# Moving one small TensorE transpose and its vector copy ahead of the projections, and writing the vector engine's two halves of a layernorm as one loop

## The reference

```python
xn = _layernorm(x, axis=-1)
x = x + _L0_attn_ref(xn, ...) + _L0_ffn_ref(xn, ...)
xn = _layernorm(x, axis=-1)
x = x + _L1_attn_ref(xn, ...) + _L1_ffn_ref(xn, ...)
# layers 2 and 3 likewise

# _L1_attn_ref, what the stage around the change prepares:
q = x @ Wq + bq
k = x @ Wk + bk
v = x @ Wv + bv
alpha = jax.nn.sigmoid(x @ Wa + ba)
beta = jax.nn.sigmoid(x @ Wb + bb)
gate = jax.nn.sigmoid(x @ Wg + bg)
# then a gated delta rule, step by step over 256 positions, and y = o @ Wo + bo

# _L1_ffn_ref: top-1 routing to 8 experts with a capacity; dropped tokens go to expert 0
final_e = _route(tokens, router_w)
for e in range(E):
    h = jax.nn.relu(tokens @ W1[e] + b1[e])
    y = h @ W2[e] + b2[e]
    out = out + jnp.where((final_e == e)[:, None], y, 0.0)
```

## Time and profile before

| what | value |
|---|---|
| median of the runs | 704.36 us |
| the three runs | 696.79, 704.61, 704.36 us |
| the profiled execution's own time | 696.79 us |
| its span, first to last instruction | 695.1 us |
| what lies around the span | 1.7 us |
| mean granted TensorE clock | 0.961 of full speed |
| instructions | 9324 |

### The profile page before, as it was taken

The page is one execution under the profiler, slowest core; times in us unless marked ns, Lnnn a source line. Parts: engine busy times, 40 slices in busy tenths (PEclk is TensorE's granted clock), DMA queues, the critical chain, the costliest instruction groups (busy, mean ns, idle before and its releaser), DMA issues. The chain is left out here.

```text
span 695.1 us, 9324 instructions
## 1 busy us (share of the span) xinstructions
PE 593.8 (85%) x3108; PEld 395.0 (57%) x3108; DVE 464.7 (67%) x816; ACT 385.2 (55%) x798; POOL 372.0 (54%) x290
## 2 busy tenths in 40 slices
PE   5999888799898996776697759896999989898887
PEld 2433444355464553555456637896889867555546
DVE  6798699899899986974455497642335655355633
ACT  3689799779898853242579834322212346323350
POOL 0678598989999872875510172957305710112220
PEclk9999799999999999999799998999999999999999
DMA  4043154346577402000240011416013100000002
GB/s 119 4 117 61 30 122 79 113 117 129 119 121 136 121 8 69 0 0 1 81 127 1 1 25 23 137 46 172 21 39 71 32 1 1 0 1 0 1 0 62
DMA packets 45673, 40.14 MB, mean 58 GB/s; under 512 B 12167, under 2 KB 32569, under 8 KB 45626
## 3 DMA queue, kind: packets, MB, share of 16 engines
q1 hardware_dynamic: 44602, 37.45, 23.4%
q0 software_dynamic: 1024, 2.10, 1.0%
HBM read 33.44 MB, written 6.09 MB: 57 GB/s over the span
## 5 line engine op out<-in xcount | busy, mean ns | idle before, releaser
L407 PE MATMUL bank<-l0s_ring,all_ident 128*128 128x512 f32 x256 | 121.0, 606 | 2.6 <-POOL l0s_ring L661 2.6
L792 DVE TENSOR_TENSOR_SCAN l0s_ring<-l_XM,l0s_carry,bank 128x512 f32<-128x512 f32 x62 | 74.6, 1258 | 8.1 <-PE bank L390 7.3
L661 POOL TENSOR_TENSOR l0s_ring<-l0s_ring,l0s_c_rest 128x1024 f32<-128x1024 f32 x32 | 67.9, 2137 | 14.0 <-DVE l0s_ring L792 9.6
L407 PEld LDWEIGHTS bank<-l0s_ring,all_ident 128*128 128x128 f32 x256 | 46.4, 195 | 48.7 <-issue 41.0
L548 ACT ACTIVATE all_XNT<-l_wraw,l_wins 128x256 f32<-128x256 f32 x160 | 67.8, 495 | 9.6 <-PE bank L390 9.5
L661 POOL TENSOR_TENSOR l0s_ring<-l0s_ring,all_XF 128x1024 f32<-128x1024 f32 x31 | 64.2, 2082 | 8.0 <-DVE l0s_ring L792 7.3
L390 PEld LDWEIGHTS bank<-all_ident,all_XNT 128*128 128x128 f32 x320 | 37.7, 143 | 31.9 <-issue 17.6
L527 ACT ACTIVATE l_XM<-l_DT,l_negA 128x512 f32<-128x512 f32 x80 | 52.7, 709 | 0.0
L390 PE MATMUL bank<-all_ident,all_XNT 128*128 128x128 f32 x320 | 43.6, 278 | 7.9 <-ACT all_XNT L548 4.7
L792 DVE TENSOR_TENSOR_SCAN l0s_ring<-bank,l0s_carry,l0s_ring 128x512 f32<-128x512 f32 x34 | 41.8, 1263 | 1.8 <-POOL l0s_ring L651 1.8
L651 POOL TENSOR_TENSOR l0s_ring<-l_DTU,l0s_b_all 128x1024 f32<-128x1024 f32 x19 | 38.0, 1999 | 0.0
(11 more groups left out here) (421 smaller groups left out, 1498.6 us busy)
## 6 DMA issues: line engine op xcount, KB each, us to landing
l0s_c_rest<-bc_rows SPq DMA_DIRECT2D x16, 512.0 KB, 5.6
all_XF<-bc_rows SPq DMA_DIRECT2D x16, 512.0 KB, 5.5
l0s_b_all<-bc_rows SPq DMA_DIRECT2D x19, 256.0 KB, 6.6
l_wall<-in_L_ffn_W SPq DMA_DIRECT2D x14, 256.0 KB, 4.6
all_X<-in_L_attn_x SPq DMA_DIRECT2D x4, 256.0 KB, 3.7
gx<-l1m_TD SPq DMA_DIRECT2D x1, 1024.0 KB, 5.6
gy<-l1m_TD SPq DMA_DIRECT2D x1, 1024.0 KB, 8.5
out<-all_X SPq DMA_DIRECT2D x4, 256.0 KB, 2.3
```

The source lines that it names most:

```text
L407: last = nc.tensor.matmul(bank_y[j][:, :], S.ident[:, :], hc[n % CRING][:, j, :], start=False, stop=(n % DS == DS - 1))
L661: nc.gpsimd.tensor_tensor(hc[n % CRING][:, :, :], h[n % RING][:, :, :], wide(c_wide[p % HRING][:, n % 2, :]), ALU.mult).then_inc(hc_ready, 1)
L792: nc.vector.tensor_tensor_scan(h[n % RING][:, j, :], factor, added, before, ALU.mult, ALU.add).then_inc(h_ready, 1)
```

## The change

On TensorE the transpose of the expert bias rows moves, with its two waits, ahead of `turn(0)`. On VectorE the helper functions go; the two halves are one loop, in which each half does its additions, its moments and its scale and shift before the next half begins. The copies of the router weights and of the wide bias now stand inside half 0, between its moments and its shift. The copy of the expert bias leaves the loop of 16 additions and stands ahead of it.

```diff
@@ block.tensor
                         nc.tensor.matmul(S.bank[6][:, 0:KVC], S.ones[0:1, :], brow[0:1, :], start=True, stop=True).then_inc(wide, 1)
+                        pe.wait_ge(E.zero_loaded, 80)
+                        pe.wait_ge(bwide_ready, 1)
+                        nc.tensor.transpose(bank_b[:, 0:NE * FE], brows, S.ident[0:NE * FE, 0:NE * FE]).then_inc(b_turned, 1)
                         turn(0)
                         turn(1)
                         pe.wait_ge(x_ready, NBLK)
...
                         keys(1)
-                        pe.wait_ge(E.zero_loaded, 80)
-                        pe.wait_ge(bwide_ready, 1)
-                        nc.tensor.transpose(bank_b[:, 0:NE * FE], brows, S.ident[0:NE * FE, 0:NE * FE]).then_inc(b_turned, 1)
                         turn(3)
@@ block.vector
-                        add_rows(0)
-                        add_rows(1)
-                        moments(0)
-                        add_rows(2)
-                        shifts(0)
-                        add_rows(3)
-                        moments(1)
-                        dve.wait_ge(rw_turned, 1)
-                        nc.vector.tensor_copy(wt[:, KVC - NE:KVC], S.bank[7][:, 0:NE]).then_inc(wt_ready, 1)
-                        dve.wait_ge(wide, 1)
-                        nc.vector.tensor_copy(bwide, S.bank[6][:, 0:KVC]).then_inc(bwide_ready, 1)
-                        shifts(1)
+                        for h in range(2):
+                            for b in (2 * h, 2 * h + 1):
+                                dve.wait_ge(add_turned, b + 1)
+                                nc.vector.tensor_tensor(S.X[:, quads(b), :], S.X[:, quads(b), :], S.bank[b][:, :].rearrange("p (k d) -> p k d", k=TPB),
+                                                        ALU.add).then_inc(x_ready, 1)
+                            for b in (2 * h, 2 * h + 1):
+                                dve.wait_ge(x_ready, b + 1)
+                                for t in range(b * TPB, (b + 1) * TPB):
+                                    last = nc.vector.bn_stats(stats[:, t, :], S.X[:, t, :])
                             last.then_inc(stats_ready, 1)
                             dve.wait_ge(stats_ready, h + 1)
...
                             last.then_inc(moments_ready, 1)
+                            if h == 0:
+                                dve.wait_ge(rw_turned, 1)
+                                nc.vector.tensor_copy(wt[:, KVC - NE:KVC], S.bank[7][:, 0:NE]).then_inc(wt_ready, 1)
+                                dve.wait_ge(wide, 1)
+                                nc.vector.tensor_copy(bwide, S.bank[6][:, 0:KVC]).then_inc(bwide_ready, 1)
                             dve.wait_ge(root_ready, h + 1)
...
+                        dve.wait_ge(b_turned, 1)
+                        nc.vector.tensor_copy(E.b1[:, :], bank_b[:, 0:NE * FE]).then_inc(b_ready, 1)
                         dve.wait_ge(bwide_ready, 1)
                         for t in range(CH):
-                            if t == 2 * TPB:
-                                dve.wait_ge(b_turned, 1)
-                                nc.vector.tensor_copy(E.b1[:, :], bank_b[:, 0:NE * FE]).then_inc(b_ready, 1)
                             dve.wait_ge(kv_done, t + 1)
```

More of the change, by code:

```diff
@@ L1605, in moments @@
                             last.then_inc(moments_ready, 1)
-                        def shifts(h):
+                            if h == 0:
[3 more added lines that the diff above has]
+                                nc.vector.tensor_copy(bwide, S.bank[6][:, 0:KVC]).then_inc(bwide_ready, 1)
                             dve.wait_ge(root_ready, h + 1)
```

## The result

| | before | after |
|---|---|---|
| median over 22 runs each | 699.20 us | 703.53 us |
| lowest and highest | 694.47 and 708.26 | 699.43 and 707.31 |
| the profiled execution | 696.79 (span 695.1) | 705.77 (span 704.0) |
| mean granted TensorE clock there | 0.961 | 0.944 |

The ratio is 1.0065, with a 95% interval from 1.0044 to 1.0087. That is +4.5 us on 699.2 (between 3.1 and 6.1): slower, and within the 2% that I called no change. The forecast was +4.7 us on 704.36, a ratio of 1.0067.

A forecast was written before the change was run, and what follows sets the result against it. The stage was taken as bound first by loads and layernorm, then by TensorE's projections. copy_x(0) later +4.30, transpose gone -0.24, clock +0.6 gave +4.7 us on 704.36: 709.0 us, range 701 to 714.

The forecast's parts named there:

- VectorE's hold: VectorE's shift of half 0, behind two copies' waits: ScalarE starts normalising 3.58 us later; alone it makes copy_x(0) 2.98 later.
- TensorE's wait: Bias transpose ahead of turn(0) waits for all five expert loads until 348.07; copy_x(0) 4.30 us later, overlapping VectorE's delay.
- the rival of an early release: Five expert loads land before TensorE's tiles are ready at 346.61; VectorE's hold decides, +3.3 us, median 707.7; chance 0.10.
- The transpose taken out of the stream: Between keys(1) and turn(3) TensorE loses the 0.24 us transpose, in a stretch without a gap: -0.24 us.
- The clock: TensorE's clock steps to full 4.7 us after it resumes, at 352.8; 1.1 us more at half speed, about +0.6 us.
- The case of a clock low on into the router's part: Clock stays low into the router's part, 10 of 125 us after 357: over 2% slower (14.1 us); chance 0.04.
- Passing on: Behind the stage no wait absorbs the delay; +4.7 us passes on whole, the profiled execution going from 696.79 to 701.5.
- The case of time given back by the clock: Later clock falls at L1283 and L2613 miss TensorE's work, giving back 3.6 us: +0.5 us, median 704.9; chance 0.12.
- The absolute time: Whole kernel: median of the runs shown 704.36 + 4.7 = 709.1, predicted as 709.0 us; the forecast's chance 0.68.
- The low end of my range: Whole kernel: 701 us, if the runs after lie at the level of the profiled execution with +4.7.

The follow-up runs named there:

- e2: Changed kernel with TensorE's order put back, leaving VectorE's part alone; ratio to before 1.0038 (1.0006 to 1.0071).
- e3: Changed kernel with the bias rows' load on its own semaphore, TensorE's transpose waiting for that load and bwide_ready; ratio to before 1.0041 (1.0005 to 1.0077).
- e1: Kernel before with TensorE's part alone: bias transpose and its two waits ahead of turn(0); ratio to before 1.0058 (1.0024 to 1.0091).
- e6: Changed kernel with TensorE also waiting for 16 very small later loads ahead of the bias transpose; ratio to before 1.0063 (1.0039 to 1.0086).
- a1_null_after: Changed kernel run again with no edit; ratio to before 1.0096 (1.0073 to 1.0119).
- n1_null: Kernel before run again with no edit; ratio to before 0.999 (0.995 to 1.003).
- e4: Kernel of e1 with the bias rows' load on its own semaphore, VectorE's order of before; ratio to before 1.000 (0.997 to 1.003).
- e10: Kernel of e3 with GpSimd's addition at L1238 waiting for half 1's shift; ratio to before 1.0048 (1.0020 to 1.0076).
- e9: Kernel before with q and g loads and the bias rows' load on own semaphores, first matmuls waiting for nine loads; ratio to before 0.999 (0.996 to 1.002).
- e7: Kernel of e3 with the two copies moved behind half 0's shift; ratio to before 1.0070 (1.0033 to 1.0107).

## Why the prediction was right in the change and wrong in the time

**VectorE's hold (forecast: ScalarE starts 3.58 later; 2.98 alone).** Shown. ScalarE's start is +8.72 in the changed kernel, 3.49 later than the 5.23 of before. Alone it moves `copy_x(0)` by 2.8 (e2, e3).

**TensorE's wait (forecast: release at 348.07, `copy_x(0)` 4.30 later, hiding VectorE's hold).** Shown. The release is at +12.09 against the +11.92 forecast, and `copy_x(0)` is 4.46 later against 4.30. e1 gives the same without VectorE's part, e3 takes it away with the loads, e6 makes it longer with a later load. The load into `KD` took 5.2 us from issue to landing in the changed kernel. The prediction's estimate of 2.2 us from the Trainium skill (DMA: Bandwidth & Descriptors, section "Anatomy of one DMA — SWDGE (gpsimd) path") does not hold for this load, which SyncE issues at the end of a series, and the rival of an early release falls with it. (Counted from the start of each issue, as the rows are, the estimate for all loads would have been 345.7 and not 346.2; that changes nothing.) The row of the DMA issues of the changed kernel (KB, us from issue to landing), for the earlier trace rows:

```profile
l1at_KD<-in_L_attn_bo SPq DMA_DIRECT2D x1, 64.0 KB, 5.2
```

**The transpose taken out of the stream (forecast: -0.24).** From `copy_x(0)` to the stage's end it is 11.07 after and 11.43 before: -0.36, which is 0.12 more than forecast. In the second pair of profiles (a1_null_after, n1_null) it is 12.37 and 12.60: -0.23.

**The clock (forecast: +0.6).** This term was mis-sized: in the pair of profiles it is 0. I had counted the step from TensorE's release (4.7 us before, so 4.7 after); in the changed kernel it came 3.56 after the release, as early behind `copy_x(0)` as before. In the other profiles of the same two kernels it came 2.4 us later (n1_null, 4.6 behind `copy_x(0)`) and 2.6 us later (a1_null_after, 4.8). From `copy_x(0)` to the end the four profiles take 11.43 and 12.60 (before), 11.07 and 12.37 (after). So it moves from run to run by more than the term, and neither pair shows it moving with the change. The case of a clock low on into the router's part did not occur.

**Passing on (forecast: whole).** The measured +4.5 us (3.1 to 6.1) against +4.10 in the stage agrees. So do most of the other kernels: the stage is longer than n1_null's by 4.38 (e1), 2.86 (e2), 2.47 (e3), 0.78 (e4), 2.26 (e10) and -0.90 (e9), and the ratios on 723 us give 4.2, 2.7, 3.0, 0.1, 3.5 and -0.9. For e7 it is 2.65 against 5.1 (2.4 to 7.7), and e6 goes the other way against a1_null_after, as said there. It is not shown by single profiles, since the rest varied between 337.5 and 343.9 on one kind of chip and between 359.5 and 365.3 on the other, without any order in the edits. The case of time given back by the clock cannot be told from that either: it would be an average over runs, and that average gave nothing back.

**The absolute time (forecast 709.0, measured 703.53).** The sum was +4.7 and the measurement +4.5. That they are 0.2 apart is partly luck: the stage has +4.10, and the interval is 3 us wide. The step that failed is the base: "I add the same to the median". I took the 7.57 us between the profiled execution and the median of the three runs shown as a property of the kernel. Over 22 runs the median of before is 699.20, 2.4 above the profiled execution, and two of the three runs happened to lie in the upper part of a spread of 694 to 708. Read against 699.20, my 709.0 is 1.4% slower, twice what was measured. 699.20 + 4.7 = 703.9 would have been the forecast. The low end of my range, 701, stood for runs at the level of the profiled execution; the measured ones lie between that and my base. With three runs of 696.8, 704.6 and 704.4 the right thing was to say that the base is uncertain by some 8 us and to carry the change as a difference.

## What to carry to other kernels

A wait on a shared count waits for everything in it. Before an instruction is moved up in an in-order list, ask which loads its semaphore counts beyond the one that it reads, and look for another engine that waits on the same count: its release time is the time of the new wait. Two holds that meet at one instruction don't add, but each stays when the other is repaired (VectorE's hold in e3, where TensorE's wait is repaired; TensorE's wait in e1, where VectorE's hold is; in e7 the shift inside GpSimd's addition takes the hold's place), so one repair alone may give nothing. And forecast a difference, over a base from as many runs as there are: the spread of a single kernel was three times this effect.

## What the runs showed of the hardware that I had not expected

**An addition on GpSimd holds up small VectorE instructions.** A SCALAR_TENSOR_TENSOR of 128x8 numbers in SBUF takes 0.17 us, but 1.60, 1.53 and 2.18 us where it fell into GpSimd's addition of 2.35 us (e2, e3, e7), and each time it ended within 0.02 us of it. The addition lost nothing by it. Moving the addition away gave 0.17 back (e10). A RECIPROCAL inside the same addition (352.52 in e2) kept its 0.20. The Trainium skill (SBUF — State Buffer, section "Who interferes with whom") says that a VectorE instruction with two SBUF inputs contends with a GpSimd instruction that reads SBUF, and one with a single input, outside what the page calls 2-port perf modes, does not. These rows agree: the shift reads the means and the scales, the reciprocal one tile. Elsewhere in the kernel before, the trace agrees only in part. VectorE and GpSimd there, 431 to 435 us, and then 407 to 411 us:

```profile
432.81 0.94 DVE L1680 SCALAR_TENSOR_TENSOR l1m_kept<-l1m_rk,l1m_other 128x16 f32<-128x16 f32 x1
433.78 1.19 DVE L1681 TENSOR_SCALAR l_f<-l1m_kept 128x16 f32<-128x16 f32 x1
...
431.22 8.62 POOL L1254 TENSOR_TENSOR l1m_prep<-l1at_NWT,l1at_level 128x512 f32<-128x512 f32 x7
```

```profile
408.56 0.51 DVE L1578 TENSOR_TENSOR all_OUTF<-l_wall 128x8 f32<-128x8 f32 x4
...
407.97 2.49 POOL L1247 TENSOR_SCALAR l1at_KD<-l_KVA,l1at_kdf 128x128 f32<-128x128 f32 x4
```

Inside GpSimd's products of two tiles (L1254) an instruction with one input was held as well: 1.19 us, where one of 128x32 numbers took 0.17 at L1637. Whether it ran in such a mode no row shows. Inside GpSimd's TENSOR_SCALAR (L1247), which reads SBUF too, four VectorE products with two inputs took 0.51 us together. So in these rows VectorE is held up by GpSimd's instructions on two tiles, and not by the one on a single tile. In the changed kernel the shift escapes only since TensorE's wait puts it right behind the addition, at 353.89 = 351.54 + 2.35.

**Chips on which the same program takes 24 us more.** Of that, 13.3 us lie between the first matmul of L1391 and the first of L1407: 31.4 us in the first profile of before and in a1_null_after, 44.7 in n1_null. The timeline of TensorE in n1_null:

```profile
458.81 0.35 PE L1400 MATMUL bank<-l1at_TT,l_wall 128*128 128x128 f32 x1 [0.22 <-issue]
460.22 1.09 PE L1400 MATMUL bank<-l1at_TT,l_wall 128*128 128x128 f32 x3 [1.07 <-issue]
463.04 0.60 PE L1400 MATMUL bank<-l1at_TT,l_wall 128*128 128x128 f32 x2 [1.73 <-issue]
```

TensorE waits for no semaphore that the profile shows, only for its own issue, a few matmuls at a time. These lines had 7.2 us of such idle time in n1_null (3.5 and 3.7 at L1400 and L1398) and none in the other two; the rest of the 13.3 us I did not trace. All eight profiles from the chips with 723 us have this idle time, and none of the four from the chips with 699 us has it. It happens in the kernel before as in the others, so it is no part of the change. Its cause stays open; the stage of the change was alike on all chips, but for the place of the clock step.
